# Attention scores on 32-row strips of TensorE, with the causal cut on GpSimd, in a two-layer transformer kernel

## What is computed

```
q = gelu(rope(x @ wqr + bqr)), k = gelu(rope(x @ wkr + bkr))   # 16 heads of 8
v = gelu(x @ wkv + bkv) @ wv + bv
scores = einsum('bhqd,bhkd->bhqk', q, k) / sqrt(8)
scores = where(key > query, -inf, scores)
out = softmax(scores) @ v        # per head, then @ wo + bo
x = x + out * silu(ffn(xn))
```

## Time and profile before

| | |
|---|---|
| median of 3 runs | 2451.81 us (2451.44 to 2452.27) |
| profiled execution, its own time | 2448.52 us |
| its span (first to last instruction) | 2446.7 us |
| busy in the span | TensorE 1809.3 (74%), VectorE 1758.5 (72%), ScalarE 1062.2 (43%), GpSimd 758.0 (31%) |
| mean granted clock of TensorE | 0.870 of 2.4 GHz |
| layer 0 and the tile loop of layer 1 | 0 to 1937.1 us |
| attention | 1937.1 us to the end |

### The profile page before, as it was taken

How to read it: one execution, slowest core, us unless ns; L and a number is a source line. 1 busy time by engine, 2 the same in 40 slices (tenths; PEclk the granted TensorE clock), 3 DMA queues, 4 the chain that set the end, 5 groups by cost and what they waited for, 6 DMA issues and landing times. The chain is left out here.

```text
span 2446.7 us, 35810 instructions
## 1 busy us (share of the span) xinstructions
PE 1809.3 (74%) x10242; PEld 1356.9 (55%) x10242; DVE 1758.5 (72%) x4377; ACT 1062.2 (43%) x1765; POOL 758.0 (31%) x577
## 2 busy tenths in 40 slices
PE   1585584664845855847586089898999999999998
PEld 1353352442523533425353078888888877777776
DVE  4999999999999999999999554444444434444443
ACT  2463362453634633625453045444555344444443
POOL 2764473463635644735586000000000000000000
PEclk8797797787878877977798589999999899999999
DMA  6220020200200201202000321010110100000000
GB/s 113 51 49 9 8 42 10 34 19 5 49 10 1 49 9 16 38 5 44 5 5 5 90 44 23 18 21 15 20 22 10 48 8 14 13 13 13 13 13 11
DMA packets 140823, 60.08 MB, mean 25 GB/s; under 512 B 94599, under 2 KB 135036, under 8 KB 140668
## 3 DMA queue, kind: packets, MB, share of 16 engines
q1 hardware_dynamic: 140668, 58.24, 11.8%
HBM read 37.10 MB, written 21.10 MB: 24 GB/s over the span
## 5 line engine op out<-in xcount | busy, mean ns | idle before, releaser
L302 POOL TENSOR_TENSOR hid<-act_g,act_u 128x512 f32<-128x512 f32 x256 | 341.1, 1332 | 530.4 <-ACT act_c L380 512.7
L405 PE MATMUL pb<-xt_hi,wg_hi 128*128 128x512 f32 (+1 forms) x264 | 211.1, 800 | 208.7 <-ACT cwt L362 168.7
L306 POOL TENSOR_TENSOR hid<-hid,act_c 128x512 f32<-128x512 f32 x256 | 344.4, 1345 | 20.1
L457 PE MATMUL pb<-hid,wd 128*128 128x512 f32 x528 | 301.9, 655 | 35.2 <-POOL hid L306 33.9
L1515 DVE SCALAR_TENSOR_TENSOR l_acc<-l_pb,l_gtok,l_acc 128x128 f32<-128x128 f32 x512 | 144.3, 344 | 253.3 <-PE l_pb L1168 253.3
L1168 PE MATMUL l_pb<-l_xt,l_big 128*128 128x512 f32 (+1 forms) x1024 | 296.3, 411 | 35.0 <-DVE l_rope L1447 25.1
L1557 DVE TENSOR_REDUCE l_mrow<-l_pb 128x2 f32<-128x256 f32 (+1 forms) x256 | 137.2, 555 | 171.4 <-PE l_pb L1168 168.4
L380 ACT ACTIVATE act_g<-pb 128x512 f32<-128x512 f32 (+1 forms) x264 | 158.3, 600 | 220.9 <-PE pb L407 215.5
L1168 PEld LDWEIGHTS l_pb<-l_big,l_hid 128*128 128x128 f32 x2048 | 247.1, 192 | 10.5
L1096 ACT ACTIVATE l_hid<-l_pb,l_cols 128x512 f32<-128x512 f32 x256 | 169.4, 688 | 183.0 <-PE l_pb L1168 182.7
L1168 PE MATMUL l_pb<-l_big,l_hid 128*128 128x128 f32 x2048 | 247.9, 275 | 0.0
(11 more groups left out here) (300 smaller groups left out, 4105.4 us busy)
## 6 DMA issues: line engine op xcount, KB each, us to landing
z_scratch<-zs SPq DMA_DIRECT2D x128, 81.0 KB, 4.2
zr<-z_scratch SPq DMA_DIRECT2D x8, 1296.0 KB, 8.4
x_sb<-in_L_attn_x_dram SPq DMA_DIRECT2D x32, 64.0 KB, 3.1
g_scratch<-act_u SPq DMA_DIRECT2D x8, 256.0 KB, 2.3
y_scratch<-yo SPq DMA_DIRECT2D x8, 256.0 KB, 2.0
l_xs<-in_L_attn_x_dram SPq DMA_DIRECT2D x32, 64.0 KB, 1.9
l_ys<-y_scratch SPq DMA_DIRECT2D x128, 16.0 KB, 1.7
l_gs<-g_scratch SPq DMA_DIRECT2D x8, 256.0 KB, 3.0
```

The lines of the kernel that those rows point to most:

```text
L302: pool.tensor_tensor(hid1[:, :], g, u, ALU.mult).then_inc(s_h1, 1)
L306: pool.tensor_tensor(hid[:, p % 2, :], hid1[:, :], c, ALU.mult).then_inc(s_h, 1)
L405: pe.matmul(out, l_hi, r_hi, start=first, stop=False, skip_group_check=True)
L457: last = pe.matmul(pb[:, 4, :], wd[0:n, p, :], hid[0:n, p % 2, :], start=(p == 0), stop=(p == PAIRS), skip_group_check=True)
```

## The change

- The masked query copies go. q lies in `qr` as it comes out of the selectors, and `tiled` issues a matmul on one strip of 32 rows (`tile_position`), so that one head is taken by the rows alone, two neighbouring heads one after the other, on two strips and into two banks.
- A `max` unit covers two heads and both halves of the queries: four strip products, then four full-width masks, into banks 2 and 3. There are 8 such units in place of 16, each waits for VectorE's reading of the one before, and VectorE reduces each with two operations.
- The maxima are laid out on the same strips (`mhl`), so the subtraction is a strip product too (`minus` times `mT`). This takes eight transposes in two units (`m0`, `m1`) and two copies of 512 elements.
- `scores_t` has four strip products and four strip subtractions into banks 4 and 5, and waits for the exponential of the step before. It has no mask. GpSimd sets the causal zeros in the probabilities after the exponential (`affine_select`, 512 elements per partition, behind a product of one element), and `values` waits for GpSimd. The probabilities of all 16 heads are kept (`pt`, `pt2`).
- A pass has 15 units in place of 22. Three selector loads remain, the last of 64 KB, and one small load (`c_qmask`) goes.

The diff, cut to what the prediction speaks of; the lines that go are also in the functions above.

```diff
@@ -787,16 +787,18 @@
-        qb = [b[:, :].rearrange("p (h n) -> p h n", h=H1) for b in (big0, big1)]
-        kr = xt[0][:, :, :].rearrange("p a n -> p (a n)"), wqk[:, :, :, :].rearrange("p a j n -> p (a j n)")
+        GN = 4 * N
+        kr = [big0[:, GN * i:GN * (i + 1)] for i in range(2)]
+        qr = [big0[:, GN * (2 + i):GN * (3 + i)] for i in range(2)]
+        mT = [big1[:, GN * i:GN * (i + 1)] for i in range(2)]
...
+        def probs(u):
+
+            return (pt, pt2)[u // 4][:, u % 4, :].rearrange("p (j n) -> p j n", j=2)
...
@@ -892,18 +900,20 @@
-        UNITS = ["k"] * 2 + ["q_dve", "q_act"] + ["max0"] * 8 + ["max1"] * 8 + ["v", "mT"]
+        UNITS = ["k0", "q0", "k1", "q1"] + ["max"] * 8 + ["v", "m0", "m1"]
+        BANK = {0: 0, 1: 1, 2: 0, 3: 1, 12: 0, 13: 1, 14: 0}
+        FREED = {0: 14, 1: 13, 2: 0, 3: 1, 12: 2, 13: 3, 14: 12}
-        O_RAW, O_TB, O_NORM, O_OT, O_WO, O_END = 0, 1, 3, 5, 6, 7
+        MAX0, NM, XU, X_AT, V_AT = 4, 8, 8, 2, (7, 9, 11, 13)
+
+        O_RAW, O_TB, O_NORM, O_OT, O_WO, O_END = 0, 1, 2, 4, 5, 6
...
@@ -1039,6 +1051,19 @@
+            def cut(b, u):
+                pool.wait_ge(s_pt, b * XU + u + 1)
+                pool.wait_ge(s_turn, b * XU + u + 1)
+                pool.tensor_tensor(turnstile[:, 1:2], turnstile[:, 0:1], turnstile[:, 0:1], ALU.mult).then_inc(s_turn, 1)
+                diagonal = probs(u)[:, :, 0:2 * P]
+                pool.affine_select(diagonal, diagonal, pattern=[[0, 4], [1, P]], base=0, channel_multiplier=-1, compare_op=ALU.is_ge, fill=0.0).then_inc(s_cut, 1)
+
+            with pool.Fori(0, B) as b:
+                for u in range(XU):
+                    cut(b, u)
...
@@ -1111,31 +1136,27 @@
                 else:
-                    act.activation(mT[par][:, :], src[:, 0:N], ACT.Copy).then_inc(s_ua_act, 1)
+                    dst = (kr if u[0] == "k" else mT)[par]
+                    at = 2 * N * int(u[1])
+                    act.activation(dst[:, at:at + 2 * N], src, ACT.Copy).then_inc(s_ua_act, 1)
...
+
                 act.wait_ge(s_st, b * XU + (u + 1))
-                act.wait_ge(s_pv, b * (XU // 2) + max(u // 2 - 1, 0))
-                at = 512 * (2 + 2 * (u % 2)) + N
-                act.activation(pt[:, u % 4, :], pbf[:, at:at + 3 * N], ACT.Exp, scale=float(1.0 / np.sqrt(HD1))).then_inc(s_pt, 1)
+                if u == 0:
+                    act.wait_ge(s_pv, b * 4)
...
@@ -1260,17 +1281,40 @@
+            def tiled(out, l, r, j, start, stop):
+                rows = slice(32 * j, 32 * (j + 1))
+                return pe.matmul(out, l[rows], r[rows], start=start, stop=stop, skip_group_check=True, tile_position=(32 * j, 0))
+
             def a_unit(b, par, i):
+                u = UNITS[i]
+                if u == "max":
+                    m = i - MAX0
+                    g = m // 2
+                    if m == 0 or m == NM // 2:
+                        pe.wait_ge(*read(b, 2 * (g // 2)))
+                        pe.wait_ge(*read(b, 2 * (g // 2) + 1))
+                    if m > 0:
+                        pe.wait_ge(*read(b, i - 1))
+                    for k in range(2):
+                        for n in range(2):
+                            tiled(pb[:, 2 + n, N * k:N * (k + 1)], qr[par][:, N * g + P * k:N * g + P * (k + 1)], kr[par][:, N * g:N * (g + 1)],
+                                  2 * (m % 2) + n, k == 0, False)
+                    for k in range(2):
+                        for n in range(2):
+                            at = (N + P) * k
+                            last = mm(pb[:, 2 + n, at:at + P], ident_b[:, :], mask_b[:, :], start=False)
+                    last.then_inc(s_ua, 1)
+                    return
+                bank = pb[:, BANK[i], :]
...
@@ -1278,53 +1322,42 @@
                 else:
                     pe.wait_ge(s_mhl, b + 1)
-                    for k in range(2):
-                        last = pe.transpose(bank[:, P * k:P * (k + 1)], mhl[:, k, :].bitcast(F32), ident[:, :])
+                    for g in range(2):
+                        h = 4 * (2 * int(u[1]) + g)
+                        for k in range(2):
+                            src = mhl[:, k, h:h + 4, :].rearrange("p j c -> p (j c)").bitcast(F32)
+                            last = pe.transpose(bank[:, N * g + P * k:N * g + P * (k + 1)], src, ident[:, :])
                 last.then_inc(s_ua, 1)
...
             def scores_t(b, par, u):
 
-
+                g = u // 2
                 if u == 0:
                     pe.wait_ge(s_ua_act, (b + 1) * N_ACT)
-                    keys = N * (h // 4) + P * k
-                    out = pbf[:, bank + lo:bank + lo + N]
-                    mm(out, kr[par][:, keys:keys + P], qb[par][:, h, :], stop=False)
-                    mm(out, esel[:, h, :], mT[par][:, :], start=False, stop=False)
-                    last = mm(out[:, P * k:P * (k + 1)], mask_b[:, :], ident_b[:, :], start=False)
+                pe.wait_ge(s_pt, b * XU + u)
+                at = slice(N * g, N * (g + 1))
+                for k in (1, 0):
+                    for n in range(2):
+                        keys = N * g + P * k
+                        tiled(pb[:, 4 + n, N * (1 - k):N * (2 - k)], kr[par][:, keys:keys + P], qr[par][:, at], 2 * (u % 2) + n, k == 1, False)
+                for k in (1, 0):
+                    for n in range(2):
+                        last = tiled(pb[:, 4 + n, N * (1 - k):N * (2 - k)], minus[:, :], mT[par][:, at], 2 * (u % 2) + n, False, True)
...
-                pe.wait_ge(s_pt, b * XU + (u + 2))
-                if u == 0:
+            def values(b, par, g):
+
+                pe.wait_ge(s_cut, b * XU + 2 * (g + 1))
+                if g == 0:
...
@@ -1352,17 +1385,15 @@
 
             def both(ba, bx, bo_, pa, px, po):
-                    if bx is not None and i % 2 == 0:
-                        u = i // 2
-                        if u < XU:
-                            scores_t(bx, px, u)
-                        if u % 2 == 0 and 0 <= u - 4 < XU:
-                            values(bx, px, u - 4)
+                    if bx is not None and 0 <= i - X_AT < XU:
+                        scores_t(bx, px, i - X_AT)
+                    if bx is not None and i in V_AT:
+                        values(bx, px, V_AT.index(i))
...
@@ -1543,23 +1577,20 @@
-                dve.tensor_reduce(mrow[:, k, 2 * j:2 * j + 2], src, AX.X, ALU.max).then_inc(s_ua_dve, 1)
-                if i == NU - 3:
+                m = i - MAX0
+                dve.tensor_reduce(mrow[:, 0, 2 * m:2 * m + 2], pb[:, 2:4, 0:P], AX.X, ALU.max)
...
-                    dve.tensor_copy(mhl[:, :, 0:H1], mrow[:, :, :]).then_inc(s_mc, 1)
+                    dve.tensor_copy(mhl[:, :, :, 0], mrow[:, :, :]).then_inc(s_mc, 1)
                     dve.wait_ge(s_mc, b + 1)
-                    dve.tensor_tensor(mhl[:, :, H1:2 * H1], mrow[:, :, :], mhl[:, :, 0:H1].bitcast(F32), ALU.subtract).then_inc(s_mhl, 1)
+                    dve.tensor_tensor(mhl[:, :, :, 1], mrow[:, :, :], mhl[:, :, :, 0].bitcast(F32), ALU.subtract).then_inc(s_mhl, 1)
 
             def o_unit(b, par, n, i):
 
```

More of the change, by code:

```diff
@@ L1280, in a_unit @@
                         last = mm(bank[:, D * k:D * (k + 1)], ckv_b[:, P * k:P * (k + 1)], wv[:, :])
-                elif u[0:3] == "max":
-                    j, k = i - UNITS.index(u), int(u[3])
-                    if u == "max0" and j == 0:
-                        pe.wait_ge(*read(b, 0))
-                        pe.wait_ge(*read(b, 2))
-                    elif u == "max0" and j == XU // 2:
-                        pe.wait_ge(*read(b, 3))
-                    for m in range(2):
-                        h, out = 2 * j + m, bank[:, N * m:N * (m + 1)]
-                        mm(out, qb[par][:, h, P * k:P * (k + 1)], kr[par][:, N * (h // 4):N * (h // 4 + 1)], stop=False)
-                        last = mm(out[:, P * k:P * (k + 1)], ident_b[:, :], mask_b[:, :], start=False)
@@ L1644, in constants @@
     c["c_rep"] = rep.reshape(P, -1)
-    esel = np.zeros((P // H1, H1, H1, P), f)
-    for h in range(H1):
-        esel[0:2, h, h, :] = -1
-    c["c_esel"] = esel.reshape(P, -1)
+    minus = np.zeros((4, 32, P), f)
+    minus[:, 0:2, :] = -1
+    c["c_minus"] = minus.reshape(P, P)
     return c
```

100 lines of the change are left out of this document (45 added, 55 removed).

## The result

The changed kernel takes **2542.09 us** (median of 4 runs, 2538.21 to 2548.81) against 2452.04 us for the kernel before, measured beside it: a ratio of **1.0365** (95% interval 1.0339 to 1.0392). The forecast was 2397 us, with a range of 2371 to 2474, so the result lies outside it and on the other side. The price of rival D (clock at 1.2 GHz, 87 us more, 2539 us) is 3 us from the measured time.

The account below looks back on a forecast made before the run. TensorE was taken as the bound before, the single-buffered maxima chain through VectorE after. A pass of 7.6 + 16.1 + 2.5 + 0.3 = 26.5 us against 30.4, fourteen times, gave 55 us less: 2397 us, range 2371 to 2474.

Parts of the forecast that it names:

- rival D: Layer 1 attention: TensorE's clock stays at 1.2 GHz; 36.6 us per pass, 87 us more; chance 0.11.
- C: GpSimd's causal cut, taken as 1.33 us, is the bound; at 3.4 a pass is 35.1, 66 more; chance 0.07.
- A: The forecast itself: strip pairs overlap in layer 1 attention; pass of 26.5 us, 55 us less; chance 0.56.
- B: Strips of a pair take turns at 0.24 us; pass of 30.3 us, 20 less to 22 more; chance 0.26.
- The forecast's 0.56: Score step for two heads: four strip pairs at 0.14 us each, 0.56 us in place of 1.44.
- That step of 0.68: Maximum step for two heads: two pairs 0.28, four masks 0.30, switch 0.10; 0.68 us in place of 0.98.
- The maxima's single buffer as the bound: Each maximum step waits for VectorE's reading of the one before; turn of 2.01 us, eight times 16.1.
- The pass of 26.5 us: Repeated attention pass: start 7.6, eight turns 16.1, end 2.5, output products and final additions 0.3; against 30.4 before.

Follow-up runs that it names:

- the kernel with full rows in every pause: The changed kernel plus 64 unused full-row products a pass, ahead of the first k, two score steps and each wait for VectorE's maxima reading: 2476.82 us.
- the masks back: The changed kernel with GpSimd's causal cut undone and four full-row masks again at the end of each score step: 2565.60 us.
- fitted fillers: The changed kernel plus 41 unused full-row products a pass, only as many as each pause holds: 2426.51 us, ratio to before 0.9886.
- the kernel with strip fillers: The changed kernel plus 64 unused products a pass in TensorE's waits, each on one strip of 32 rows: 2648.67 us.
- the last kernel: The changed kernel with two maxima buffers, latent product and transposed maxima in banks 2 and 3, and 16 full-row fillers a pass: 2379.58 us, ratio to before 0.9708.

## Why the prediction was wrong

- **The clock (rival D, chance 0.11).** This is the step that failed. The forecast priced the repeated passes at 2.4 GHz, on the ground that score, q and k products stand close together at the start of the second pass, "as before". They stand there, but the clock did not rise: it was at 1.2 GHz for most of the second pass (0.53, where the kernel before had 0.89) and came back only at its end, and from then on it fell in every pass, 5 to 8 us after the first k product. The reason given for D, "the new passes have more pauses", was not the main one: with pauses and full rows the clock was 0.87 to 1.00, with strips and no pause 0.58. What the strips lack is shown by the fillers: the same number in the same places gave 1.00 on 128 rows and 0.58 on 32. In the attention of before every matmul used 128 rows, so nothing there showed what 32 would do, and that unknown should have been bounded from both sides like the others.
- **D's price** came close, in part by luck: 36.6 us a pass against 35.8, a maximum step of 1.2 us against 1.26, 2539 us against 2542.09. D had the clock down for the whole pass, where it was up for 7 to 10 us of each. In the pass that begins at 2150.24 the first maximum starts after 8.2 us (D: 10.5), the eight turns take 23.3 (23.1) and the end 4.7 (3.0). It also counted the fourteen passes alone (87 us; measured 75.9) and nothing for the first two and the end (11.6 and 5.3), and these errors all but cancel.
- **The range** left C and D out because A and B held 0.82; that followed from the chances, and D's 0.11 was too low.
- **Strips overlap (A against B): right.** The matmuls of a pair start within 0.01 us of each other, and a score step takes 0.66 us, against 0.96 over all rows. The forecast's 0.56 was too low by 0.10: a pair costs 0.12 and not 0.14, but a step that passes from full rows to strips and back pays about 0.1 each way, which the forecast charged to the maximum step alone, and once. That step of 0.68 was too low by 0.08 (0.76, within its bounds of 0.48 to 0.98). The Trainium skill's rule (TensorE: Matmul & The Clock Gate, LDWEIGHTS), by which a load goes by its columns, gave an estimated 0.85 for eight loads in turn; the trace lies below it, so by that figure loads on two strips overlap as well. A maximum step gained nothing from strips, 0.76 against 0.77: its four products went from 0.56 to 0.44, and its four masks, which then pass back to strips, from 0.21 to 0.32.
- **The maxima's single buffer as the bound: wrong in this kernel.** At 1.2 GHz TensorE's own work filled most of the turns, and a second buffer did not help (2555.04). At 2.4 GHz the turn exists: in the kernel with full rows in every pause a maximum unit that nothing else delays starts 1.95 us after the one before; the forecast had 2.01.
- **The pass of 26.5 us** was not reached with one buffer; the nearest are 28.5 at clock 1.00 with the masks back and 27.9 with fitted fillers. Both have matmuls that the changed kernel has not, so what it would take itself with the clock at 1.00 is not shown. The forecast was short there in one respect at least: score step, maximum step and value products together (0.66 + 0.76 + 0.79 = 2.21) exceed the turn; the forecast added this for B and not for A, where its own terms already gave 0.56 + 0.68 + 0.9 = 2.14 against 2.01.
- **The cut (rival C): right to be small.** 0.64 us, half the 1.33 taken; nobody waited, and its removal changed nothing.
- **Two small misreadings of the trace** changed next to nothing. Two groups, not three, follow from 2129.48 to 2130.20, and two reductions of 0.69 us that take 1.29 run into each other by 0.09, not 0.06 (the pair now takes 1.02 us, 2137.70 to 2138.72, for the 1.05 forecast).

## What to carry to other kernels

A change that moves TensorE's work to fewer rows can cost its clock: price it at both levels, and do not count matmuls on part of the rows as equal cover to full ones, even where the engine never pauses. When the clock column falls, try a few full-row matmuls with unused results in waits that exist anyway; 16 a pass, in pauses ahead of two score steps, were enough here once the buffers let the rest stand close. Only with the clock held does the removal of a wait show its worth: the second buffer lost 13 us without the fillers, while with them it is 37 us ahead of the best kernel with one (2389.08 and 2426.51; the latter also has 19 more fillers a pass).

## What the runs showed of the hardware

- TensorE busy for 44.07 of 44.30 us was granted 0.58 of its clock when 160 of its 302 matmuls used 32 rows, and 1.00 when 96 did and 64 fillers used 128. The Trainium skill (TensorE: Matmul & The Clock Gate, HAM oscillation) tells of clock lost to TensorE's idle time; the kernel before with the new waits agrees in a small way (0.87 to 1.00), and the kernel with strip fillers shows a loss almost without idle time.
- The same work was granted either level of the clock: with the masks back a pass took 28.5 or 38.2 us in one execution. Strips between full-row work ran at 1.00 in fourteen passes in a row.
- Two matmuls of 256 columns on different strips and banks cost what one does, 0.12 us at 2.4 GHz, with about 0.1 us more where the program passes between strips and full rows.

Left open: whether it is the number of rows that counts, and in proportion, or the issue by strips as such (no kernel issued matmuls on 64 rows), and whether the clock would hold if all four strips ran at once. None of this was tried. Nor was the last kernel run without its 16 fillers.
